# The last tile's products of a conditional-mix and routed low-rank layer, put in another column order

## The chip, the cores and the metric

One core of one Trainium2 chip. The metric is the device time of one execution in microseconds, the median of several. The core's engines run side by side and are tied by semaphores: TensorE (PE) multiplies, VectorE (DVE) and ScalarE (ACT) read its results, GpSimd (POOL) gathers rows, SyncE (SP) issues most transfers.

## The reference

For 64 batches, a matrix `W = weights[condition]` of 32 x 32 mixes the 32 channels of `x` (64, 32, 512). The mixed rows `y` then go through a base layer and a routed low-rank layer, and all of it is added to `x`:

```python
y      = einsum('bct,bcd->bdt', x, weights[condition])       # 64 x 32 x 512
result = einsum('bnd,od->bno', y, W_base) + b_base           # 512 -> 512
logits = einsum('bnd,ed->bne', y, W_gate)                    # 8 experts
route  = top-2 of softmax(logits), renormalised
h      = einsum('bnd,erd->bner', y, A)                       # 8 experts x 16 ranks
delta  = einsum('bner,eor->bno', h * route, B)
out    = x + result + delta
```

## The kernel before

The 2048 rows are cut into 16 tiles of 128 rows (four batches), tile 0 to tile 15 (`LAST`). For a tile, TensorE computes `y` turned, by four products of `x` with a block-diagonal matrix (`mix_tile`, L467, into `y_ps`). ACT copies it into `y_hi` (L271), a type with fewer bits, and DVE takes the rest, `y_lo` (L360). Weights are split in the same way into `w_hi` and `w_lo`. The main products are then three for each of four chunks of 128 features, `y_hi` with `w_hi`, `y_hi` with `w_lo`, and `y_lo` with `w_hi`: 12 steps, all added up in PSUM.

The columns of the weights are laid out as: 256 of the base layer's first half (`BASE`), 64 ranks (`H`), 256 of its second half, 64 ranks, 8 of the gate (`E`), 648 in all (`ALL`). A step takes them in two products, of 320 and of 328 columns (L485), into the two banks of `main_ps[t % 2]`. In this way `main_ps0` belongs to even tiles and `main_ps1` to odd ones, tiles 13 and 15 among these.

DVE routes a tile (`route_tile`: L367 top values, L369 indices, five small steps, L385 the weighted ranks `hw`). TensorE transposes `hw` (`turn`, L495, into `hwT_ps`), ACT copies it into `hwT_hi` (L282), DVE takes the rest into `hwT_lo` (L394), and TensorE adds six low-rank products of 256 columns (`lora`, L505) onto the base columns. DVE adds the bias to `x` beforehand (`add_bias`, L401) and then the sum in `main_ps` to it (`finish`, L407). SP stores the tile (L215).

The order on each engine is written out by hand. On TensorE the work of tile t - 1 stands among the products of tile t: its transposition ahead of step 4, its low-rank products ahead of step 9. The mix products of tile t + 1 stand ahead of the products of tile t. A tile's products wait for `result_ready` of the tile two before, which had the same banks.

The last tile is written apart. Its ranks and gate come first, as 12 side products of 144 columns (L565) into the free `y_ps0`, so that its route can begin early. Then come its base columns, two products of 256 to a step (L571), with the transposition of tile 14 after step 1, the transposition of tile 15 and the low-rank products of tile 14 after step 7, and at the end its own low-rank products, half by half. Two adds (L448) and two stores (L219) of half a tile end the program.

Of the kernel before, what the change touches and what calls it, by code (L numbers as in the profile page):

```python
# [5 lines left out]
def adaln_ffn_kernel(  # L6
# [20 lines left out]
    ALU = mybir.AluOpType  # L27
# [6 lines left out]
    TILES = BATCHES // Q  # L34
    CHUNKS = D // P
    RANKS = b_lora.shape[0]
    E = w_all.shape[1] - D - RANKS
# [6 lines left out]
    BASE, H, G = OUT // 2, RANKS // 2, E // 2  # L44
    HALF = BASE + H
    ALL = 2 * HALF + E
    SIDE = H + E
    LAST = TILES - 1


# [2 lines left out]
    STEPS = len(ORDER)  # L53
    TURN_AT, LORA_AT = 4, 9
    SECOND_MIX_AT = 4
    LAST_TURN_AT = 1, 7
    PICKED = 2


# [7 lines left out]
    with ctx:  # L67
# [108 lines left out]
        result_ready = sem("result_ready")  # L176
        stored = sem("stored")

        def first_halves():

            for h, bank in enumerate((y_ps[0], hwT_ps[0])):
                f = slice(h * D // 2, (h + 1) * D // 2)
                yield bank[:, 0:D // 2], y_hi[0][:, f], y_lo[0][:, f]
# [3 lines left out]
        @block.sync  # L187
        def _(sp):
            def load_x(t):
                sp.dma_start(x_sb[:, t, :], x_tiles[t, :, :]).then_inc(x_landed[t], 16)  # L190

            def load_w(c):
                sp.dma_start(w_raw[:, c, :], w_chunks[c, :, :]).then_inc(w_landed[c], 16)

            sp.dma_start(cond_sb[:, :], cond).then_inc(cond_landed, 16)  # L195
            sp.dma_start(table[:, :, :], cond_w.rearrange("(p k) d -> p k d", k=K)).then_inc(table_landed, 16)
            load_x(0)
            load_w(0)
            load_w(1)
            load_x(1)  # L200
            load_w(2)
            load_w(3)

            sp.wait_ge(mixw_landed[0], 16)
            sp.dma_start(b_raw[:, :], b_lora).then_inc(b_landed, 16)
            load_x(2)
            sp.dma_start(bias_sb[:, :], bias.to_broadcast([P, OUT])).then_inc(bias_landed, 16)
            load_x(3)
            for t in range(LAST):
                if t + 4 < TILES:  # L210

                    sp.wait_ge(y_done, t + 2)
                    load_x(t + 4)
                sp.wait_ge(result_ready, t + 1)
                sp.dma_start(out_tiles[t, :, :], x_sb[:, t, :]).then_inc(stored, 16)  # L215
            for half in range(2):
                n = slice(half * BASE, (half + 1) * BASE)
                sp.wait_ge(result_ready, LAST + half + 1)
                sp.dma_start(out_tiles[LAST, :, n], x_sb[:, LAST, n]).then_inc(stored, 16)  # L219
            sp.wait_ge(stored, 16 * (TILES + 1))  # L220

# [39 lines left out]
        @block.scalar  # L261
        def _(act):
            def split_w(c):
                act.wait_ge(w_landed[c], 16)
                act.activation(w_hi[:, c, :], w_raw[:, c, :], ACT.Copy).then_inc(w_hi_ready, 1)

            def split_y(t):
                act.wait_ge(y_done, t + 1)
                if t >= 2:
                    act.wait_ge(main_done, t - 1)  # L270
                act.activation(y_hi[t % 2][:, :], y_ps[t % 2][:, :], ACT.Copy).then_inc(y_hi_ready, 1)  # L271

            def exp_second(t):
                act.wait_ge(top_ready, t + 1)
                act.activation(second[:, :], top[:, 0:1], ACT.Exp, bias=top[:, 1:2], scale=-1.0)\  # L275
                    .then_inc(second_ready, 1)

            def split_hwT(t):
                act.wait_ge(hwT_done, t + 1)
                if t >= 2:  # L280
                    act.wait_ge(base_done, t - 1)
                act.activation(hwT_hi[t % 2][:, :], hwT_ps[t % 2][:, 0:P], ACT.Copy)\  # L282
                    .then_inc(hwT_hi_ready, 1)

            act.wait_ge(table_landed, 16)
            act.activation(table_split[:, :, 0, :], table[:, :, :], ACT.Copy).then_inc(table_hi_ready, 1)
            split_w(0)
            split_w(1)
            for (y, hi, _), done, ready in zip(first_halves(), (first_y_done, y_done),
                                               (first_y_hi_ready, y_hi_ready)):  # L290
                act.wait_ge(done, 1)
                act.activation(hi, y, ACT.Copy).then_inc(ready, 1)
            split_w(2)
            split_w(3)
            split_y(1)
            act.wait_ge(b_landed, 16)
            act.activation(b_hi[:, :], b_raw[:, :], ACT.Copy).then_inc(b_hi_ready, 1)  # L297

            for t in range(1, TILES):
                exp_second(t - 1)  # L300
                if t == LAST:
                    exp_second(LAST)
                else:
                    split_y(t + 1)
                split_hwT(t - 1)
            split_hwT(LAST)

        @block.vector
        def _(dve):
# [82 lines left out]
            def low_hwT(t):  # L392
                dve.wait_ge(hwT_hi_ready, t + 1)
                dve.tensor_tensor(hwT_lo[t % 2][:, :], hwT_ps[t % 2][:, 0:P], hwT_hi[t % 2][:, :].bitcast(f32),  # L394
                                  ALU.subtract).then_inc(hwT_lo_ready, 1)
# [31 lines left out]
            for t in range(1, TILES):  # L427
                before = main_ps[(t - 1) % 2]
                route_tile(t - 1, before[:, :, BASE:HALF], before[:, 1, HALF:HALF + E])
                if t + 2 < TILES:  # L430
                    select(t + 2)
                if t == LAST:
                    side = y_ps[0][:, 0:2 * SIDE].rearrange("p (h n) -> p h n", h=2)
                    route_tile(LAST, side[:, :, 0:H], side[:, 1, H:SIDE])
                low_hwT(t - 1)
                if t + 1 < TILES:
                    low_y(t + 1)
                add_bias(t - 1)
                if t == LAST:
                    low_hwT(LAST)  # L440
                    add_bias(LAST)
                finish(t - 1)

            dve.wait_ge(xb_ready, TILES)
            for half in range(2):
                n = slice(half * BASE, (half + 1) * BASE)
                dve.wait_ge(base_done, LAST + half + 1)
                dve.tensor_tensor(x_sb[:, LAST, n], main_ps[LAST % 2][:, half, 0:BASE], x_sb[:, LAST, n],  # L448
                                  ALU.add).then_inc(result_ready, 1)

        @block.tensor
        def _(pe):
# [20 lines left out]
                y, w = ((y_hi, w_hi), (y_hi, w_lo), (y_lo, w_hi))[n]  # L473
                return y[t % 2][:, c * P:(c + 1) * P], w[:, c, :]

            def side_columns(w):

                first = w[:, BASE:BASE + SIDE]
                return bass.AP(first.tensor, first.offset, [first.ap[0], [HALF, 2], [1, SIDE]])

            def main_step(t, i, c, n):
                y, w = operands(c, n, t)
                for half in range(2):
# [10 lines left out]
                    pe.wait_ge(hwT_lo_ready, t - 1)  # L494
                pe.transpose(hwT_ps[t % 2][:, 0:P], hw[t % 2][:, :], ident[:, :]).then_inc(hwT_done, 1)  # L495

            def lora(t, by_half=False):
                pe.wait_ge(hwT_lo_ready, t + 1)
                parts = ((hwT_hi, b_hi), (hwT_hi, b_lo), (hwT_lo, b_hi))
                order = [(n, half) for n in range(3) for half in range(2)]  # L500
                if by_half:
                    order.sort(key=lambda x: x[1])
                for n, half in order:
                    h, w = parts[n]
                    last = pe.matmul(main_ps[t % 2][:, half, 0:BASE], h[t % 2][:, :],  # L505
                                     w[:, half * BASE:(half + 1) * BASE],
                                     start=False, stop=n == 2, skip_group_check=True)
                    if (n, half) == order[-1] or by_half and n == 2:
                        last.then_inc(base_done, 1)

            pe.wait_ge(warm_ready, 1)
            warm_up(WARM_BEFORE)
# [45 lines left out]
                    main_step(t, i, c, n)  # L558


            pe.wait_ge(y_lo_ready, TILES)
            side = y_ps[0][:, 0:2 * SIDE].rearrange("p (h n) -> p h n", h=2)
            for i, (c, n) in enumerate(ORDER):
                y, w = operands(c, n, LAST)
                last = pe.matmul(side, y, side_columns(w), start=i == 0, stop=i == STEPS - 1)  # L565
            last.then_inc(main_done, 1)
            pe.wait_ge(result_ready, LAST - 1)
            for i, (c, n) in enumerate(ORDER):
                y, w = operands(c, n, LAST)
                for half in range(2):  # L570
                    pe.matmul(main_ps[LAST % 2][:, half, 0:BASE], y, w[:, half * HALF:half * HALF + BASE],  # L571
                              start=i == 0, stop=i == STEPS - 1)
                if i == LAST_TURN_AT[0]:
                    turn(LAST - 1)
                if i == LAST_TURN_AT[1]:
                    turn(LAST)
                    lora(LAST - 1)
            lora(LAST, by_half=True)


# [33 lines left out]
```

## Time and profile before

| | |
|---|---|
| median of 3 runs | 97.9 us (97.78 to 98.39) |
| the profiled execution | 97.5 us, of which the span of its trace is 95.7 |
| TensorE busy | 90.5 us, 95% of the span |
| DVE busy | 65.6 us, 69% |
| ACT busy | 23.8 us, 25% |
| GpSimd busy | 16.1 us, 17% |
| moved by DMA | 10.65 MB, 111 GB/s over the span |

Busy time of TensorE is counted from modelled ends of its matmuls, which overlap; so its pace is read from the spacing of the matmuls' starts, or from the pieces of the chain of waits. That chain is followed back from the last instruction: at each step to whatever released it, or to the instruction ahead of it on its engine.

### The profile page before, as it was taken

The numbers are of one execution on the slowest core, as the hardware profiler recorded it, in microseconds if no ns is written. First come the engines' busy times: TensorE is split into PE (matmuls) and PEld (weight loads), VectorE is DVE, ScalarE is ACT, GpSimd is POOL, SyncE is SP. The second block draws the span as 40 slices with busy tenths as digits, with TensorE's granted clock in tenths as the row PEclk, the third lists the DMA queues.
The fourth block names the chain that finished last, engine by engine and source line by source line (L and its number), as shares of the span: only waits on it lengthen the run. The fifth ranks groups of instructions, "written<-read, shape, count | busy, mean of one in ns | idle before, by whom it ended". The sixth has DMA issues, their size and how long they took to land.

```text
span 95.7 us, 1847 instructions
## 1 busy us (share of the span) xinstructions
PE 90.5 (95%) x657; PEld 87.6 (92%) x657; DVE 65.6 (69%) x234; ACT 23.8 (25%) x56; POOL 16.1 (17%) x29
## 2 busy tenths in 40 slices
PE   5997998999999999999999999999999999999980
PEld 1387997999999999999999999999999999999970
DVE  3768957767586686767675866867676767668880
ACT  5138433130403131221304031311313040311300
POOL 4384303030303021030303030120300000000000
PEclk9999999999999999999999999999999999999999
DMA  0895483060606233140606051331607020302005
GB/s 13 252 335 218 173 265 124 9 219 9 219 7 147 79 132 101 73 153 0 226 7 219 7 188 38 115 115 52 176 8 219 0 110 0 116 0 110 0 10 209
DMA packets 6361, 10.65 MB, mean 111 GB/s; under 512 B 1009, under 2 KB 1617, under 8 KB 6353
## 3 DMA queue, kind: packets, MB, share of 16 engines
q1 hardware_dynamic: 5904, 10.32, 32.6%
q0 software_dynamic: 448, 0.23, 1.1%
q8 instruction: 5, 0.08, 0.4%
q14 instruction: 4, 0.02, 0.1%
HBM read 6.35 MB, written 4.19 MB: 110 GB/s over the span
## 4 chain that ended last, share of the span: by engine, by line
PE 81%; DMA 10%; DVE 2%; issue 1%; ACT 1%; POOL 0%; SPq 0%; DVEq 0%; POOLq 0%
PE main_ps L485 51%; PE y_ps L467 12%; PE main_ps L505 12%; DMA mixw<-cond_w,row_ids 5%; PE main_ps L571 3%; DMA b_raw<-b_lora 3%; DMA table<-cond_w 2%; PE hwT_ps L495 2%; PE y_ps L565 1%; ACT b_hi L297 1%; POOL table_split L238 0%; DVE x_sb L448 0%; SPq L195 0%; DVE hw L385 0%; DVEq L67 0%
## 5 line engine op out<-in xcount | busy, mean ns | idle before, releaser
L485 PE MATMUL main_ps<-w_lo,y_hi 128*128 128x320 f32 x120 | 28.8, 321 | 0.0
L485 PE MATMUL main_ps<-w_hi,y_hi 128*128 128x320 f32 x120 | 28.8, 320 | 0.0
L485 PE MATMUL main_ps<-w_hi,y_lo 128*128 128x320 f32 x120 | 27.4, 311 | 0.0
L242 POOL DMA_INDIRECT mixw<-cond_w,row_ids x14 | 13.7, 976 | 49.3 <-PE y_ps L467 48.6
L485 PEld LDWEIGHTS main_ps<-w_hi,y_lo 128*128 128x128 f32 x120 | 20.3, 188 | 0.0
L485 PEld LDWEIGHTS main_ps<-w_lo,y_hi 128*128 128x128 f32 x120 | 19.9, 189 | 0.1
L485 PEld LDWEIGHTS main_ps<-w_hi,y_hi 128*128 128x128 f32 x120 | 19.4, 190 | 0.0
L467 PE MATMUL y_ps<-mix,x_sb 128*128 128x128 f32 x124 | 16.6, 276 | 0.6 <-DMA x_sb<-x 0.5
L467 PEld LDWEIGHTS y_ps<-mix,x_sb 128*128 128x128 f32 x124 | 15.6, 191 | 0.8 <-issue 0.7
L275 ACT ACTIVATE second<-top 128x1 f32<-128x1 f32 x16 | 4.7, 296 | 44.3 <-DVE top L367 44.3
L407 DVE TENSOR_TENSOR x_sb<-main_ps,x_sb 128x512 f32<-128x512 f32 x15 | 10.4, 691 | 5.7 <-PE main_ps L505 5.7
L394 DVE TENSOR_TENSOR hwT_lo<-hwT_ps,hwT_hi 128x128 fp32r<-128x128 f32 x16 | 4.7, 292 | 12.8 <-ACT hwT_hi L282 12.8
L401 DVE TENSOR_TENSOR x_sb<-x_sb,bias_sb 128x512 f32<-128x512 f32 x16 | 10.9, 682 | 0.0
L271 ACT ACTIVATE y_hi<-y_ps 128x512 fp32r<-128x512 f32 x15 | 9.0, 598 | 5.5 <-PE y_ps L467 5.5
L360 DVE TENSOR_TENSOR y_lo<-y_ps,y_hi 128x512 fp32r<-128x512 f32 x15 | 10.2, 681 | 0.0
L282 ACT ACTIVATE hwT_hi<-hwT_ps 128x128 fp32r<-128x128 f32 x16 | 4.4, 278 | 10.6 <-PE hwT_ps L495 10.5
L505 PE MATMUL main_ps<-b_hi,hwT_hi 128*128 128x256 f32 x32 | 6.6, 284 | 0.0
L505 PE MATMUL main_ps<-b_hi,hwT_lo 128*128 128x256 f32 x32 | 6.6, 283 | 0.0
L505 PE MATMUL main_ps<-b_lo,hwT_hi 128*128 128x256 f32 x32 | 6.6, 282 | 0.0
L385 DVE SCALAR_TENSOR_TENSOR hw<-main_ps,weight,route 128x128 f32<-128x128 f32 x15 | 5.3, 351 | 0.6
L455 PE MATMUL hwT_ps<-warm 128*128 128x512 bf16 (+1 forms) x12 | 4.3, 484 | 1.2 <-DVE warm L310 1.2
L505 PEld LDWEIGHTS main_ps<-b_hi,hwT_hi 128*128 128x128 f32 x32 | 5.4, 188 | 0.0
(66 smaller groups left out, 77.8 us busy)
## 6 DMA issues: line engine op xcount, KB each, us to landing
x_sb<-x SPq DMA_DIRECT2D x16, 256.0 KB, 2.9
out<-x_sb SPq DMA_DIRECT2D x15, 256.0 KB, 2.0
w_raw<-w_all SPq DMA_DIRECT2D x4, 324.0 KB, 4.6
b_raw<-b_lora SPq DMA_DIRECT2D x1, 256.0 KB, 2.8
bias_sb<-bias SPq DMA_DIRECT2D x1, 256.0 KB, 4.5
out<-x_sb SPq DMA_DIRECT2D x2, 128.0 KB, 1.8
mixw<-cond_w,row_ids POOLq DMA_INDIRECT x14, 2.4
table<-cond_w SPq DMA_DIRECT2D x1, 64.0 KB, 2.0
```

What stands on the lines that cost most here:

```text
L242: pool.indirect_dma_start(mixw[:, t, :], None, cond_w, bass.IndirectOffsetOnAxis(row_ids[:, t:t + 1], 0))\
L271: act.activation(y_hi[t % 2][:, :], y_ps[t % 2][:, :], ACT.Copy).then_inc(y_hi_ready, 1)
L275: act.activation(second[:, :], top[:, 0:1], ACT.Exp, bias=top[:, 1:2], scale=-1.0)\
L282: act.activation(hwT_hi[t % 2][:, :], hwT_ps[t % 2][:, 0:P], ACT.Copy)\
L360: dve.tensor_tensor(y_lo[t % 2][:, :], y_ps[t % 2][:, :], y_hi[t % 2][:, :].bitcast(f32), ALU.subtract).then_inc(y_lo_ready, 1)
L385: dve.scalar_tensor_tensor(out=hw[t % 2][:, :].rearrange("p (h e r) -> p h e r", h=2, e=G), in0=h.rearrange("p h (e r) -> p h e r", e=G), ...
L394: dve.tensor_tensor(hwT_lo[t % 2][:, :], hwT_ps[t % 2][:, 0:P], hwT_hi[t % 2][:, :].bitcast(f32), ALU.subtract).then_inc(hwT_lo_ready, 1)
L401: dve.tensor_tensor(x_sb[:, t, :], x_sb[:, t, :], bias_sb[:, :], ALU.add).then_inc(xb_ready, 1)
L407: dve.tensor_tensor(tile, main_ps[t % 2][:, :, 0:BASE], tile, ALU.add)\
L467: last = pe.matmul(dst, x_sb[:, t, f], mix[t % 2][:, :, :], start=True, stop=True)
L485: last = pe.matmul(main_ps[t % 2][:, half, 0:n_cols], y, w[:, half * HALF:half * HALF + n_cols], start=i == 0, stop=i == STEPS - 1)
L505: last = pe.matmul(main_ps[t % 2][:, half, 0:BASE], h[t % 2][:, :], w[:, half * BASE:(half + 1) * BASE], start=False, stop=n == 2, skip_gr ...
```

## The change

The last tile's 12 steps are done twice, over other columns. In the first pass a step is one product of 392 columns (64 ranks, the second half of the base, 64 ranks, gate) into the second bank of `main_ps1`; in the second pass one of 256 columns (first half of the base) into the first bank. So there are 24 products and not 36, and no column is computed twice. `y_ps0` is no longer used by the last tile. The wait on `result_ready` stands ahead of the first pass. The transposition of tile 14 stands before step 10 of the first pass, the low-rank products of tile 14 before step 5 of the second pass, the transposition of tile 15 before the second pass's last step.

The tile's own low-rank products begin with the second half, and the third of a half alone waits for `hwT_lo`. The last adds and stores take the second half first. On DVE the bias of tile 12 and 13 is added in the turn of tile 13, that of tiles 14 and 15 in the turn of tile 14; the low part of tile 14's `hwT` is taken ahead of the route of tile 15, and the low part of tile 15's behind the sum of tile 14. (DVE's turn t is the pass of its loop that works on tile t - 1's route; "turn of tile 14" is the one that takes `y_lo` of tile 15.)

```diff
@@ sync @@
-            for half in range(2):
+            for i, half in enumerate((1, 0)):
                 n = slice(half * BASE, (half + 1) * BASE)
-                sp.wait_ge(result_ready, LAST + half + 1)
+                sp.wait_ge(result_ready, LAST + i + 1)
                 sp.dma_start(out_tiles[LAST, :, n], x_sb[:, LAST, n]).then_inc(stored, 16)
@@ vector @@
+                low_hwT(t - 1)
                 if t == LAST:
-                    side = y_ps[0][:, 0:2 * SIDE].rearrange("p (h n) -> p h n", h=2)
-                    route_tile(LAST, side[:, :, 0:H], side[:, 1, H:SIDE])
-                low_hwT(t - 1)
+                    route_tile(LAST, last_ranks, last_side[:, SIDE - E:SIDE])
                 if t + 1 < TILES:
                     low_y(t + 1)
-                add_bias(t - 1)
-                if t == LAST:
-                    low_hwT(LAST)
+                if t < LAST - 1:
+                    add_bias(t - 1)
+                if t == LAST - 2:
+                    add_bias(LAST - 2)
+                if t == LAST - 1:
+                    add_bias(LAST - 1)
                     add_bias(LAST)
                 finish(t - 1)
 
+            low_hwT(LAST)
@@ tensor @@
             pe.wait_ge(y_lo_ready, TILES)
-            side = y_ps[0][:, 0:2 * SIDE].rearrange("p (h n) -> p h n", h=2)
-            for i, (c, n) in enumerate(ORDER):
-                y, w = operands(c, n, LAST)
-                last = pe.matmul(side, y, side_columns(w), start=i == 0, stop=i == STEPS - 1)
-            last.then_inc(main_done, 1)
             pe.wait_ge(result_ready, LAST - 1)
             for i, (c, n) in enumerate(ORDER):
                 y, w = operands(c, n, LAST)
-                for half in range(2):
-                    pe.matmul(main_ps[LAST % 2][:, half, 0:BASE], y, w[:, half * HALF:half * HALF + BASE],
-                              start=i == 0, stop=i == STEPS - 1)
-                if i == LAST_TURN_AT[0]:
+                if i == LAST_TURN_AT:
                     turn(LAST - 1)
-                if i == LAST_TURN_AT[1]:
+                last = pe.matmul(last_side, y, w[:, BASE:ALL], start=i == 0, stop=i == STEPS - 1)
+            last.then_inc(main_done, 1)
+            for i, (c, n) in enumerate(ORDER):
+                y, w = operands(c, n, LAST)
+                if i == LAST_LORA_AT:
+                    lora(LAST - 1)
+                if i == OWN_TURN_AT:
                     turn(LAST)
-                    lora(LAST - 1)
-            lora(LAST, by_half=True)
+                pe.matmul(last_base[0], y, w[:, 0:BASE], start=i == 0, stop=i == STEPS - 1)
+            pe.wait_ge(hwT_hi_ready, TILES)
+            for half in (1, 0):
+                n = slice(half * BASE, (half + 1) * BASE)
+                pe.matmul(last_base[half], hwT_hi[LAST % 2][:, :], b_hi[:, n], start=False, stop=False,
+                          skip_group_check=True)
+                pe.matmul(last_base[half], hwT_hi[LAST % 2][:, :], b_lo[:, n], start=False, stop=False,
+                          skip_group_check=True)
+                pe.wait_ge(hwT_lo_ready, TILES)
+                pe.matmul(last_base[half], hwT_lo[LAST % 2][:, :], b_hi[:, n], start=False, stop=True,
+                          skip_group_check=True).then_inc(base_done, 1)
```

On TensorE, at the seam between tile 14 (`y_hi0`, `main_ps0`) and tile 15 (`y_hi1`, `main_ps1`), before:

```order
L485 MATMUL main_ps0<-w_hi,y_lo0 128x328
L565 MATMUL y_ps0<-w_hi,y_hi1 128x144 [waits y_lo_ready]
L565 MATMUL y_ps0<-w_lo,y_hi1 128x144
...
L565 MATMUL y_ps0<-w_hi,y_lo1 128x144
L571 MATMUL main_ps1<-w_hi,y_hi1 128x256 [waits result_ready]
L571 MATMUL main_ps1<-w_hi,y_hi1 128x256
```

And now:

```order
L490 MATMUL main_ps0<-w_hi,y_lo0 128x328
L568 MATMUL main_ps1<-w_hi,y_hi1 128x392 [waits result_ready,y_lo_ready]
L568 MATMUL main_ps1<-w_lo,y_hi1 128x392
...
L568 MATMUL main_ps1<-w_hi,y_hi1 128x392
L500 MATMUL hwT_ps0<-ident,hw0 128x128 [waits hwT_lo_ready,hw_ready]
L568 MATMUL main_ps1<-w_lo,y_hi1 128x392
```

The wait on `result_ready` has moved from behind the twelve side products to the head of the tile.

On TensorE, around tile 15's own transposition (`hw1`), before:

```order
L495 MATMUL hwT_ps1<-ident,hw1 128x128 [waits hwT_lo_ready,hw_ready]
L505 MATMUL main_ps0<-b_hi,hwT_hi0 128x256 [waits hwT_lo_ready]
...
L571 MATMUL main_ps1<-w_hi,y_lo1 128x256 x2
L571 MATMUL main_ps1<-w_hi,y_hi1 128x256 x2
L571 MATMUL main_ps1<-w_lo,y_hi1 128x256 x2
L571 MATMUL main_ps1<-w_hi,y_lo1 128x256 x2
L505 MATMUL main_ps1<-b_hi,hwT_hi1 128x256 [waits hwT_lo_ready]
```

And now:

```order
L576 MATMUL main_ps1<-w_lo,y_hi1 128x256
L500 MATMUL hwT_ps1<-ident,hw1 128x128 [waits hwT_lo_ready,hw_ready]
L576 MATMUL main_ps1<-w_hi,y_lo1 128x256
L580 MATMUL main_ps1<-b_hi,hwT_hi1 128x256 [waits hwT_hi_ready]
L582 MATMUL main_ps1<-b_lo,hwT_hi1 128x256
L585 MATMUL main_ps1<-b_hi,hwT_lo1 128x256 [waits hwT_lo_ready]
```

Between the transposition and the products that need its result fourteen products stood, and one stands now.

On DVE, from `y_lo` of tile 15 (`y_lo1`) on, now:

```order
L402 TENSOR_TENSOR hwT_lo1<-hwT_ps1,hwT_hi1 128x128 [waits hwT_hi_ready]
L368 TENSOR_TENSOR y_lo1<-y_ps1,y_hi1 128x512 [waits y_hi_ready]
L409 TENSOR_TENSOR x_sb<-x_sb,bias_sb 128x512 [waits y_done] x2
L415 TENSOR_TENSOR x_sb<-main_ps1,x_sb 128x512 [waits xb_ready,base_done]
L375 MAX top<-main_ps0 128x8 [waits second_ready,main_done]
```

Before, one bias add (L401) stood where two stand now, ahead of the add that empties tile 13 out of `main_ps1`.

## Rows read from the trace of the kernel before

**Rows 1.** The page: the span, busy time by engine, TensorE's granted clock in 40 slices

```profile
span 95.7 us, 1847 instructions
PE 90.5 (95%) x657; PEld 87.6 (92%) x657; DVE 65.6 (69%) x234; ACT 23.8 (25%) x56; POOL 16.1 (17%) x29
...
PEclk9999999999999999999999999999999999999999
```

**Rows 2.** The chain of waits, 82 us on: start us, us, what

```profile
83.98 1.49 PE main_ps L485 x10
...
87.08 1.30 PE y_ps L565 x12
...
89.01 1.41 PE main_ps L571 x12
...
92.56 0.03 issue
```

**Rows 3.** TensorE's timeline: start us, us, engine line operation out<-in [idle before <-releaser]

```profile
86.92 0.23 PE L565 MATMUL y_ps<-w_hi,y_hi 128*128 128x144 f32 x1
...
90.26 0.27 PE L495 MATMUL hwT_ps<-ident,hw 128*128 128x128 f32 x1
...
92.03 0.28 PE L505 MATMUL main_ps<-b_hi,hwT_hi 128*128 128x256 f32 x1
...
92.62 0.28 PE L505 MATMUL main_ps<-b_hi,hwT_lo 128*128 128x256 f32 x1
```

**Rows 4.** DVE's timeline, 84.5 us on

```profile
84.54 0.68 DVE L360 TENSOR_TENSOR y_lo<-y_ps,y_hi 128x512 fp32r<-128x512 f32 x1
85.14 0.68 DVE L401 TENSOR_TENSOR x_sb<-x_sb,bias_sb 128x512 f32<-128x512 f32 x1
86.23 0.69 DVE L407 TENSOR_TENSOR x_sb<-main_ps,x_sb 128x512 f32<-128x512 f32 x1 [0.41 <-PE main_ps L505]
87.12 0.17 DVE L367 MAX8 top<-main_ps 128x8 f32<-128x8 f32 x1 [0.20 <-PE main_ps L485]
...
88.16 0.35 DVE L385 SCALAR_TENSOR_TENSOR hw<-main_ps,weight,route 128x128 f32<-128x128 f32 x1
...
89.72 0.28 DVE L394 TENSOR_TENSOR hwT_lo<-hwT_ps,hwT_hi 128x128 fp32r<-128x128 f32 x1
89.92 0.68 DVE L401 TENSOR_TENSOR x_sb<-x_sb,bias_sb 128x512 f32<-128x512 f32 x1
90.88 0.29 DVE L394 TENSOR_TENSOR hwT_lo<-hwT_ps,hwT_hi 128x128 fp32r<-128x128 f32 x1 [0.28 <-ACT hwT_hi L282]
...
92.65 0.76 DVE L448 TENSOR_TENSOR x_sb<-main_ps,x_sb 128x256 f32<-128x256 f32 x2 [0.28 <-PE main_ps L505]
```

**Rows 5.** ACT's timeline, tile 15's copy of the transposed ranks

```profile
90.57 0.28 ACT L282 ACTIVATE hwT_hi<-hwT_ps 128x128 fp32r<-128x128 f32 x1 [1.24 <-PE hwT_ps L495]
```

**Rows 6.** Tile 1: timelines of DVE and TensorE around the transposition of tile 0's ranks

```profile
14.52 0.35 DVE L385 SCALAR_TENSOR_TENSOR hw<-main_ps,weight,route 128x128 f32<-128x128 f32 x1
...
14.93 0.33 PE L495 MATMUL hwT_ps<-ident,hw 128*128 128x128 f32 x1 [0.45 <-DVE hw L385]
```

**Rows 7.** SP's timeline: the stores of tiles 13, 14 and of the two halves

```profile
86.95 0.33 SPq L215 DMA_DIRECT2D out<-x_sb  x1
...
92.40 0.33 SPq L215 DMA_DIRECT2D out<-x_sb  x1
...
93.10 0.33 SPq L219 DMA_DIRECT2D out<-x_sb  x1
...
93.48 0.45 SPq L219 DMA_DIRECT2D out<-x_sb  x1
```

**Rows 8.** DMA, GB/s in 40 slices: of 86 to 90 us, of 92.6 to 95.2; landing times

```profile
GB/s 0 0 0 0 0 0 0 0 0 0 0 0 0 0 0 0 0 102 328 369 389 389 410 389 226 21 0 0 0 0 0 0 0 0 0 0 0 0 0 0
...
GB/s 0 0 0 0 0 0 0 0 0 189 221 378 410 410 410 347 378 378 410 284 268 221 378 331 331 347 237 95 142 284 362 362 362 299 190 48 0 0 0 0
...
out<-x_sb SPq DMA_DIRECT2D x2, 128.0 KB, 1.8
```

More of the change, by code:

```diff
@@ L46, in adaln_ffn_kernel @@
     ALL = 2 * HALF + E
-    SIDE = H + E
+    SIDE = H + BASE + H + E
     LAST = TILES - 1
@@ L55, in adaln_ffn_kernel @@
     SECOND_MIX_AT = 4
-    LAST_TURN_AT = 1, 7
+    LAST_TURN_AT, LAST_LORA_AT, OWN_TURN_AT = 10, 5, 11
     PICKED = 2
@@ L177, in adaln_ffn_kernel @@
         stored = sem("stored")
+        last_base = [main_ps[LAST % 2][:, 0, 0:BASE], main_ps[LAST % 2][:, 1, H:H + BASE]]
+        last_side = main_ps[LAST % 2][:, 1, 0:SIDE]
+        first_ranks = last_side[:, 0:H]
+        last_ranks = bass.AP(first_ranks.tensor, first_ranks.offset, [first_ranks.ap[0], [H + BASE, 2], [1, H]])
         def first_halves():
@@ L300, in _ @@
                 exp_second(t - 1)
-                if t == LAST:
-                    exp_second(LAST)
-                else:
+                if t < LAST:
                     split_y(t + 1)
                 split_hwT(t - 1)
+            exp_second(LAST)
             split_hwT(LAST)
@@ L431, in _ @@
                     select(t + 2)
+                low_hwT(t - 1)
                 if t == LAST:
-                    side = y_ps[0][:, 0:2 * SIDE].rearrange("p (h n) -> p h n", h=2)
-                    route_tile(LAST, side[:, :, 0:H], side[:, 1, H:SIDE])
-                low_hwT(t - 1)
+                    route_tile(LAST, last_ranks, last_side[:, SIDE - E:SIDE])
                 if t + 1 < TILES:
                     low_y(t + 1)
-                add_bias(t - 1)
-                if t == LAST:
-                    low_hwT(LAST)
+                if t < LAST - 1:
[4 more added lines that the diff above has]
+                    add_bias(LAST - 1)
                     add_bias(LAST)
                 finish(t - 1)
+            low_hwT(LAST)
             dve.wait_ge(xb_ready, TILES)
-            for half in range(2):
+            for i, half in enumerate((1, 0)):
                 n = slice(half * BASE, (half + 1) * BASE)
-                dve.wait_ge(base_done, LAST + half + 1)
-                dve.tensor_tensor(x_sb[:, LAST, n], main_ps[LAST % 2][:, half, 0:BASE], x_sb[:, LAST, n],
-                                  ALU.add).then_inc(result_ready, 1)
+                dve.wait_ge(base_done, LAST + i + 1)
+                dve.tensor_tensor(x_sb[:, LAST, n], last_base[half], x_sb[:, LAST, n], ALU.add).then_inc(result_ready, 1)
         @block.tensor
@@ L474, in operands @@
                 return y[t % 2][:, c * P:(c + 1) * P], w[:, c, :]
-            def side_columns(w):
-                first = w[:, BASE:BASE + SIDE]
-                return bass.AP(first.tensor, first.offset, [first.ap[0], [HALF, 2], [1, SIDE]])
             def main_step(t, i, c, n):
@@ L495, in turn, with lora @@
                 pe.transpose(hwT_ps[t % 2][:, 0:P], hw[t % 2][:, :], ident[:, :]).then_inc(hwT_done, 1)
-            def lora(t, by_half=False):
+            def lora(t):
                 pe.wait_ge(hwT_lo_ready, t + 1)
[L499 to L509, printed above, removed]
+                for n, (h, w) in enumerate(((hwT_hi, b_hi), (hwT_hi, b_lo), (hwT_lo, b_hi))):
+                    for half in range(2):
+                        last = pe.matmul(main_ps[t % 2][:, half, 0:BASE], h[t % 2][:, :],
+                                         w[:, half * BASE:(half + 1) * BASE],
+                                         start=False, stop=n == 2, skip_group_check=True)
+                last.then_inc(base_done, 1)
             pe.wait_ge(warm_ready, 1)
@@ L569, in _ @@
                 y, w = operands(c, n, LAST)
-                for half in range(2):
-                    pe.matmul(main_ps[LAST % 2][:, half, 0:BASE], y, w[:, half * HALF:half * HALF + BASE],
-                              start=i == 0, stop=i == STEPS - 1)
-                if i == LAST_TURN_AT[0]:
+                if i == LAST_TURN_AT:
                     turn(LAST - 1)
-                if i == LAST_TURN_AT[1]:
-                    turn(LAST)
-                    lora(LAST - 1)
-            lora(LAST, by_half=True)
+                last = pe.matmul(last_side, y, w[:, BASE:ALL], start=i == 0, stop=i == STEPS - 1)
[5 more added lines that the diff above has]
+                if i == OWN_TURN_AT:
+                    turn(LAST)
+                pe.matmul(last_base[0], y, w[:, 0:BASE], start=i == 0, stop=i == STEPS - 1)
[9 more added lines that the diff above has]
+                          skip_group_check=True).then_inc(base_done, 1)
 def kernel(**inputs):
```

## The prediction

> **What bounds the kernel now.** I read the page first: TensorE (PE) is busy 95% of a span of 95.7 us, at a granted clock of full speed, which is the 2.4 GHz level [rows 1]. The chain of waits then says whether that busy time is also the path, and from 82 us on it is: matmuls follow matmuls without a hole until 92.56, and only then come the VectorE (DVE) adds and the stores [rows 2]. So in the stage that the change rewrites, a microsecond off TensorE's queue is a microsecond off the end, and a microsecond that TensorE stands still is one on it. What TensorE waits for, or nearly waits for, is read from the timelines of TensorE, DVE and ScalarE (ACT) in the last 11 us [rows 3, 4, 5].
>
> From the chain I also take the prices. Ten main products of 324 columns on average take 1.49 us, 0.149 each; twelve of 256 columns take 1.41, 0.1175 each; and the twelve side products of 144 columns take 1.30, 0.108 each [rows 2]. The low-rank products have 256 columns too, so six take 0.71. The side products are dear for their width: 144 columns cost nearly what 256 do. Their spacing is that of the weight load, which I therefore price at 0.11 where nothing hides it. A transposition takes 0.11 of the queue in the chain's pieces.
>
> **Sum, part one: the products.** Before, the last tile costs 12 side products (1.30) and 24 of 256 columns (24 x 0.1175 = 2.82, and 0.05 of unevenness), 4.17 in all: from 86.92 to the start of the tile's first low-rank product at 92.03 there are 5.11 us, less two transpositions (0.22) and the six low-rank products of tile 14 (0.71) [rows 2, 3]. After, there are 12 products of 392 columns and 12 of 256. No row has 392 columns. Low bound: no dearer than 324 columns, 0.149. High bound: the slope between 256 and 324 columns, (0.149 - 0.1175) / 68 = 0.00046 a column, carried on for 68 more, 0.181. I take 0.179, since that slope is measured right beside it. That gives 12 x 0.179 + 12 x 0.1175 = 2.15 + 1.41 = 3.56. **Gain 0.61** (low-bound price: 0.97).
>
> The Trainium skill (TensorE: Matmul & The Clock Gate, Back-to-back issue gap) gives N/2.4 + 2.5 ns for an isolated stream, 0.166 for 392 columns and 0.109 for 256. The row for 256 columns shows 0.1175, so this case's trace is dearer than the rule. An estimate by the page alone would make the twelve wide products 0.16 us cheaper than my sum.
>
> **Part two: a wait at the head of the tile.** The side products went to y_ps, which was free, so TensorE went from tile 14 to tile 15 without waiting for anything, and the wait on result_ready stood behind them, long fulfilled. Now the first product writes main_ps1, so it waits for the add that empties tile 13 out of it. Before, that add ran from 86.23 for 0.69, to 86.92 [rows 4]: already just when TensorE wants to start. And it is now later. In tile 14's turn DVE has two bias adds ahead of it in place of one. They are 0.60 apart (84.54, 85.14), so the second starts at 85.74 and the emptying add at 86.34 instead of 86.23; the idle 0.41 before it hides most of the extra add, not all. It ends at 87.03. From DVE's end to TensorE's weight load takes 0.06 (in tile 1 hw ends at 14.87 and TensorE, which stood waiting for it, starts at 14.93 [rows 6]), and the load is exposed, 0.11. First product at 87.20 instead of 86.92: **loss 0.28**. Bounds: 0.11 if the load were hidden and the semaphore free, 0.4 if both are dearer than in tile 1. The same second bias in tile 13's turn costs nothing: between the emptying add and the next tile's max TensorE is what DVE waits for, and TensorE has four mix products (0.9 us) before it needs that result. Queued behind the stalled load are all of the tile's products and both transpositions.
>
> **Part three: DVE's chain, moved.** Tile 14's transposition goes behind ten wide products: 87.20 + 1.79 = 88.99. Its operand hw is ready at 88.51 [rows 4], so no wait. ACT starts 0.31 after a transposition (90.26, 90.57) and DVE's hwT_lo 0.31 after that (90.88) [rows 3, 4, 5]: 89.61. The route of tile 15 now stands behind hwT_lo. It starts 0.20 later, 89.81 (its logits are there at 89.67: last wide product at 89.28, and the 0.39 that lie between a product's start and DVE's at the end, 92.26 to 92.65), and takes 1.39 (87.12 to 88.51), to 91.20; with 0.06, TensorE can load it at 91.26. TensorE meanwhile: the base products start at 88.99 + 0.11 + 2 x 0.179 = 89.46; five of them, six low-rank, six more end at 91.46, and the load for the transposition is wanted one product sooner, 91.34. **No wait, but only 0.08 to spare.** The two bias adds that have left this stretch cost nothing here, before or now; DVE is not the path.
>
> **Part four: the tail.** Before, twelve products stood between tile 15's transposition (90.26) and its own low-rank products (92.03), so ACT and DVE had 1.77 us. Now one product stands there. Transposition 91.46, ACT 91.77 to 92.05, load 92.11, product 92.22; TensorE would be free at 91.69: **loss 0.53**. Then two products, and the third needs hwT_lo: DVE starts at 92.08, 0.29, so 92.37, 0.06, 0.11: 92.54 against 92.46, **loss 0.08**. Bounds for the two together: 0.4 (load hidden) to 0.8. The rest of the order within the tail (b_hi, b_lo, then the low part, half 1 first) costs nothing: the same six products.
>
> **TensorE together**: 0.28 - 0.61 + 0.53 + 0.08 = +0.28; the last product starts at 92.89 instead of 92.62 [rows 3]. What TensorE no longer does, it waits.
>
> **Part five: the stores.** The first half's add starts 0.39 after its last product's start (three products ahead of the one at 92.62, so 92.26, and the add at 92.65), the store goes out 0.45 later, and SP's second store 0.38 behind the first: 93.10 and 93.48 before [rows 3, 4, 7]; now 93.38 and 93.76, **+0.28**. The second add would be ready at 93.68, so SP's pace decides, as before. But the queue is emptier. Before, the store of tile 14 went out at 92.40, and the three streamed in one piece of some 1.7 us, to about 94.9, 1.42 after the last issue [rows 7, 8]. Now tile 14's sum needs the low-rank products that are through at 90.9, and DVE is free at 91.12; its store goes out at 91.8 and is over by 93.5. Alone, a store flows 0.8 after its issue, and 256 KB take 0.8 (87.8 to 88.6 [rows 8]), so 128 KB 0.4 to 0.5: done 1.25 to 1.3 after the issue. **Gain 0.13** (bounds 0 and 0.2). All stores: +0.28 - 0.13 = **+0.15**.
>
> The Trainium skill (DMA: Bandwidth & Descriptors, Anatomy of one DMA — SWDGE (gpsimd) path) puts a constant 2.0 us plus bytes / 436 GB/s on a DMA, mostly the write's receipt, 2.3 for 128 KB. The rows have 1.8 at the median from issue to landing for the halves, behind another store, so that constant is not seen here; an estimate by the rule would leave the gain of 0.13 out, which is the third rival below.
>
> The profiled execution took 97.5 (95.7 of span, 1.8 around it), 0.4 under the median of 97.9. The difference carries over: 97.65 for such an execution, **98.05 for the median, said as 98.0**. About 1% (0.98 us) is what a measurement of this kernel can tell from no change.
>
> **Rivals.** (1) The first wait doesn't bite, because the semaphore comes through before TensorE has drained: 0.28 less, 97.75. Against it: the add ended at 86.92 even without the second bias. Chance 0.10. (2) The tail is hidden too, TensorE never stands: 0.61 less, 97.4. It would need ACT's copy within 0.23 of the transposition; the rows have 0.59. 0.05. (3) The stores get no cheaper: 98.2. For it: the two halves follow each other in the queue as before. 0.14. (4) Slower: DVE's route of tile 15 comes late at its transposition. It decides from 0.08. Route never yet read one bank of main_ps while TensorE wrote the other; if its seven instructions take a third longer, 0.46, then 0.38 pass on, 98.4. Against: the two routes here read different tensors, and the first took 1.39 [rows 4], with TensorE writing another tensor throughout. 0.08. (5) The clock falls to 1.2 GHz in the new gaps: some 10,800 columns of the last tile at 0.42 ns more, +4.5, 102. Against: in tile 1 TensorE stood 0.45 us and the clock stayed at full speed [rows 1, 6]. 0.02. That the change doesn't do what it says is excluded by the order. The forecast holds 0.61.
>
> **Range.** The low prices of the wide products (-0.36) or rival 2 give 97.4 to 97.7; rivals 3 and 4 and the high ends of the waits reach 98.5. 97.4 to 98.5 leaves out about 2 in 10. Faster by over 1% (under 96.9) needs rival 2 and the low price together, 0.03; slower by over 1% (over 98.9) rival 5 or a large rival 4, 0.06; within 1%, 0.91.
>
> **What would show it.** TensorE's timeline: first 392-column product at 87.2, 0.28 behind its predecessor's natural slot, with DVE's emptying add as its releaser; spacing 0.179; an idle stretch of about 0.5 before L580 with ACT's hwT_hi as releaser; last product 92.9. DVE: two bias adds before the emptying add of tile 13; tile 14's sum near 91.1. SP: stores at 91.8, 93.4, 93.8. Wrong it would be if the wide products took 0.15 or less, or if TensorE waited for hw at the last transposition.

## The result, and the profile after

| | before | after |
|---|---|---|
| median of 22 runs each | 97.83 us | 98.28 us |
| span of the profiled execution | 95.7 | 96.2 |
| TensorE busy | 90.5 | 90.6 |
| tile 13's transposition to the start of the last product | 8.91 | 9.23 |
| from there to the end of the span | 3.08 | 3.08 |

The ratio is 1.0049, 95% interval 1.0025 to 1.0072: slower by 0.24 to 0.70 us, within the 1% that was called no change, and inside the range of 97.4 to 98.5. One of the 22 executions after took 115.8 us at a mean granted clock of 0.77; it is left out of the ratio, and the last 9 us, which the change rewrites, are too short to lose 18 us even at half the clock. The forecast difference was +0.15, which lies just below the interval; the part on the prediction says which of its terms did that.

The last two lines of the table are the measures used below. In the first 15 us an execution's length varies for reasons outside the change: over ten profiled executions of ten kernels the first transposition began anywhere from 14.55 to 15.74 us, while from there to tile 13's it always took 68.7 to 68.9. So an effect of 0.1 is read from tile 13's transposition on (83.71 before, 83.89 after), not from the span. Of the span's 0.5 us, 0.18 lie ahead of that point and have nothing to do with the last tile; 0.32 lie behind it. How far such a stretch varies by itself, pairs of kernels with the same order on TensorE show: 8.91 and 8.91 (before and before_bias), 9.23 and 9.23 (after and store_act), 8.30 and 8.30 (late_ranks and late_act), each pair within 0.01.

The page after, its span and busy time by engine:

```profile
span 96.2 us, 1824 instructions
PE 90.6 (94%) x645; PEld 87.2 (91%) x645; DVE 65.4 (68%) x234; ACT 23.8 (25%) x56; POOL 15.9 (17%) x29
```

Twelve products fewer, and TensorE is busy as long as before [rows 1]. The busy time hides the gain because matmuls overlap and their ends are modelled. The chain of waits shows it, piece by piece (start us, us, what):

```profile
86.37 0.90 PE main_ps L490 x6
87.27 0.08 issue
87.34 2.02 PE main_ps L568 x10
89.36 0.11 PE hwT_ps L500
89.47 0.36 PE main_ps L568 x2
...
91.14 0.72 PE main_ps L576 x6
91.86 0.12 PE hwT_ps L500
...
92.00 0.29 ACT hwT_hi L291
...
92.33 0.38 PE main_ps L580
92.72 0.11 PE main_ps L582
92.83 0.23 PE main_ps L585
```

Before, this chain was TensorE without a hole [rows 2]. Now an "issue" stands at 87.27, ACT is on the chain at 92.00, and the piece of ten wide products is 2.02 long though nine spacings of 0.177 and one product are 1.77: the first of them carries a wait. TensorE's timeline at the three places:

```profile
86.81 0.46 PE L490 MATMUL main_ps<-w_hi,y_lo 128*128 128x320 f32 x2
87.34 0.42 PE L568 MATMUL main_ps<-w_hi,y_hi 128*128 128x392 f32 x1
87.60 0.34 PE L568 MATMUL main_ps<-w_lo,y_hi 128*128 128x392 f32 x1
...
91.70 0.27 PE L500 MATMUL hwT_ps<-ident,hw 128*128 128x128 f32 x1
...
92.33 0.38 PE L580 MATMUL main_ps<-b_hi,hwT_hi 128*128 128x256 f32 x1 [0.25 <-ACT hwT_hi L291]
92.55 0.28 PE L582 MATMUL main_ps<-b_lo,hwT_hi 128*128 128x256 f32 x1
92.67 0.38 PE L585 MATMUL main_ps<-b_hi,hwT_lo 128*128 128x256 f32 x1
92.88 0.28 PE L580 MATMUL main_ps<-b_hi,hwT_hi 128*128 128x256 f32 x1
...
93.12 0.28 PE L585 MATMUL main_ps<-b_hi,hwT_lo 128*128 128x256 f32 x1
```

A product that follows a wait is longer in the record (0.42 for 0.34, 0.38 for 0.28), since it is shown from about when its weights start to load; and the idle time in brackets, 0.25, is counted from a modelled end. So the length of a wait is best read forward: the start of the product behind, less one spacing, is where the waiting product really ran. The second wide product starts at 87.60, so the first ran at 87.42; its natural slot was 0.149 behind the last narrow one, 87.10. **Lost 0.32.** In the same way L580 ran at 92.43 and its slot was 91.92: **lost 0.51**. The third low-rank product ran at 92.76 and not at 92.67: **0.09**.

DVE's timeline, to be held against [rows 4] (`hw` of tile 15 is the operand of its transposition):

```profile
85.31 1.28 DVE L409 TENSOR_TENSOR x_sb<-x_sb,bias_sb 128x512 f32<-128x512 f32 x2
86.51 0.69 DVE L415 TENSOR_TENSOR x_sb<-main_ps,x_sb 128x512 f32<-128x512 f32 x1
...
90.02 0.17 DVE L375 MAX8 top<-main_ps 128x8 f32<-128x8 f32 x1
...
91.05 0.35 DVE L393 SCALAR_TENSOR_TENSOR hw<-main_ps,weight,route 128x128 f32<-128x128 f32 x1
...
92.31 0.29 DVE L402 TENSOR_TENSOR hwT_lo<-hwT_ps,hwT_hi 128x128 fp32r<-128x128 f32 x1 [0.32 <-ACT hwT_hi L291]
```

Two bias adds in place of one, no idle time ahead of the emptying add, which ends at 87.20. TensorE's next weight load follows 0.11 later:

```profile
87.31 0.19 PEld L568 LDWEIGHTS main_ps<-w_hi,y_hi 128*128 128x128 f32 x1 [0.32 <-issue]
```

The gain is there as well. From 87.42 to L580's slot at 91.92 are 4.50 us; less two transpositions (0.22) and the low-rank products of tile 14 (0.71) the two passes take 3.57, against the 4.17 of before by the prediction's account: 0.60 saved. 0.32 + 0.51 + 0.09 less 0.60 is the 0.32 of the table.

### The profile page after: what moved, and what is told of

It reads as the page before. It is cut to its first block, busy times and chain, and to the rows that moved or that the text cites. A ratio compares the mean times of both kernels' runs of the same rounds, so it can differ in the third digit from the quotient of the medians.

```text
span 96.2 us, 1824 instructions
## 1 busy us (share of the span) xinstructions
PE 90.6 (94%) x645; PEld 87.2 (91%) x645; DVE 65.4 (68%) x234; ACT 23.8 (25%) x56; POOL 15.9 (17%) x29
## 4 chain that ended last, share of the span: by engine, by line
PE 81%; DMA 10%; DVE 2%; issue 2%; ACT 1%; POOL 0%; SPq 0%; DVEq 0%; POOLq 0%
PE main_ps L490 51%; PE y_ps L477 12%; PE main_ps L506 11%; DMA mixw<-cond_w,row_ids 5%; DMA b_raw<-b_lora 3%; PE main_ps L568 2%; DMA table<-cond_w 2%; PE hwT_ps L500 2%; PE main_ps L576 1%; ACT b_hi L306 1%; POOL table_split L247 0%; DVE x_sb L459 0%; PE main_ps L580 0%; SPq L204 0%; DVE hw L393 0%
## 5 line engine op out<-in xcount | busy, mean ns | idle before, releaser
L506 PE MATMUL main_ps<-b_hi,hwT_lo 128*128 128x256 f32 x30 | 6.0, 283 | 0.0
L506 PE MATMUL main_ps<-b_hi,hwT_hi 128*128 128x256 f32 x30 | 6.0, 282 | 0.0
L506 PE MATMUL main_ps<-b_lo,hwT_hi 128*128 128x256 f32 x30 | 6.0, 282 | 0.0
```

## The experiments

All were timed beside the kernel before on the same chip; the stretches are from one profiled execution each.

| kernel | ratio to before, 95% | tile 13's transposition to last product | from there to the end |
|---|---|---|---|
| before | | 8.91 | 3.08 |
| after | 1.0049 (1.0025 to 1.0072) | 9.23 | 3.08 |
| wait_only | 1.0009 (0.9969 to 1.0049) | 9.14 | 3.08 |
| free_bank | 0.9988 (0.9952 to 1.0024) | 8.90 | 3.07 |
| bias_back | 1.0019 (0.9991 to 1.0047) | 9.19 | 3.08 |
| late_ranks | 0.9952 (0.9923 to 0.9980) | 8.30 | 3.10 |
| turn_10 | 0.9986 (0.9941 to 1.0031) | 9.11 | 3.08 |
| store_act | 0.9984 (0.9939 to 1.0030) | 9.23 | 2.99 |
| before_bias | 1.0000 (0.9956 to 1.0044) | 8.91 | 3.07 |
| late_act | 0.9945 (0.9917 to 0.9974) | 8.30 | 3.05 |

Only the change itself and the two "late" kernels move the time by more than its interval. For the others the stretches decide, and the ratios only say that nothing else of size happened.

**wait_only: the wait alone, in the kernel before**

```diff
             pe.wait_ge(y_lo_ready, TILES)
+            pe.wait_ge(result_ready, LAST - 1)
             side = y_ps[0][:, 0:2 * SIDE].rearrange("p (h n) -> p h n", h=2)
...
             last.then_inc(main_done, 1)
-            pe.wait_ge(result_ready, LAST - 1)
```

> The kernel before with one line moved: the wait on result_ready stands ahead of the twelve side products, which still write y_ps0. Measure: from tile 13's transposition to the start of the last product, 8.91 us before and 9.23 after. Theory (the wait at the head of the tile costs its full length, because TensorE is the path): the emptying add ends as before, 0.1 to 0.12 later the weights load, 0.11 for the load: 0.2 to 0.25 later, so 9.11 to 9.16, and the time 0.2 to 0.25 us longer. Rival (the hole is absorbed by slack behind it): 8.91 and no difference.

9.14. DVE's emptying add and TensorE's weight load for the first side product:

```profile
86.67 0.69 DVE L407 TENSOR_TENSOR x_sb<-main_ps,x_sb 128x512 f32<-128x512 f32 x1 [0.41 <-PE main_ps L505]
...
87.48 0.19 PEld L566 LDWEIGHTS y_ps<-w_hi,y_hi 128*128 128x128 f32 x1 [0.22 <-issue]
```

The add ends at 87.36 and the load begins at 87.48. The 0.23 of this hole stands in full at the last product: nothing behind it absorbs it. The wait at the head of a tile costs even where the add in question isn't late.

**bias_back: one bias add ahead of the emptying add, in the changed kernel**

```diff
+                if t == LAST:
+                    add_bias(LAST - 1)
+                    add_bias(LAST)
                 low_hwT(t - 1)
...
-                if t < LAST - 1:
+                if t < LAST:
                     add_bias(t - 1)
-                if t == LAST - 2:
-                    add_bias(LAST - 2)
-                if t == LAST - 1:
-                    add_bias(LAST - 1)
-                    add_bias(LAST)
```

> The changed kernel with one bias add in tile 14's turn, as before, and those of tiles 14 and 15 in DVE's idle stretch ahead of the low part of tile 14's hwT. Theory: the second bias add is 0.11 of the first wait of 0.32, so 9.12; if the two adds end later than ACT's hwT_hi, up to 0.1 of that comes back at the transposition. Rival (the add's place is of no account, the wait is all the emptying add): 9.23.

9.19, between the 9.12 of the theory and the rival's 9.23, for the reason that the theory had named. From tile 13's transposition to tile 14's it took 5.21 and not 5.31: the second bias add was 0.10 of the first wait. But 0.07 of it came back by tile 15's transposition (7.77 against 7.80). The chain has it in the low-rank products of tile 14, a piece of 0.72 after (at 90.42), and DVE's timeline shows why (the last line is the chain's):

```profile
89.18 1.28 DVE L409 TENSOR_TENSOR x_sb<-x_sb,bias_sb 128x512 f32<-128x512 f32 x2
90.38 0.28 DVE L402 TENSOR_TENSOR hwT_lo<-hwT_ps,hwT_hi 128x128 fp32r<-128x128 f32 x1
...
90.91 0.79 PE main_ps L504 x6
```

The two adds fill what was idle time, and `hwT_lo` starts when they let it, without a wait for ACT; it ends at 90.66, and the first low-rank product of tile 14, which waits for it, has its turn on TensorE at 90.75, less than the 0.16 that a weight load and its wait take. The adds were moved from one place with 0.1 too little room to another.

**free_bank: the wide pass in a bank that nobody has to empty**

```diff
-        last_base = [main_ps[LAST % 2][:, 0, 0:BASE], main_ps[LAST % 2][:, 1, H:H + BASE]]
-        last_side = main_ps[LAST % 2][:, 1, 0:SIDE]
+        last_base = [main_ps[LAST % 2][:, 0, 0:BASE], y_ps[0][:, H:H + BASE]]
+        last_side = y_ps[0][:, 0:SIDE]
...
             pe.wait_ge(y_lo_ready, TILES)
-            pe.wait_ge(result_ready, LAST - 1)
...
             last.then_inc(main_done, 1)
+            pe.wait_ge(result_ready, LAST - 1)
```

> The changed kernel with the 392-column products in y_ps0 instead of main_ps1's second bank, and the wait on result_ready between the two passes. Theory: the first wait (0.32) is gone and everything behind keeps its distances, since only 0.14 of slack lies at tile 15's transposition: 9.23 less 0.32 is 8.91, the time that of the kernel before, ratio 1.000. Rival (DVE's chain sets the time of tile 15's transposition, not TensorE's queue): hw of tile 14 or the order on DVE takes the gain back, 9.1 or more.

8.90, the stretch of the kernel before, and a time that can't be told from it. The chain, from the head of the tile and at the tail:

```profile
87.85 1.77 PE y_ps L567 x10
...
92.27 0.29 ACT hwT_hi L291
...
92.60 0.39 PE y_ps L580
```

Ten wide products now take 1.77 where they took 2.02, and no wait stands ahead of them. The tail is unchanged. So the whole loss against the kernel before is the first wait, and the wait in the tail alone eats what the products save.

**turn_10: tile 15's transposition one product sooner**

```diff
-    LAST_TURN_AT, LAST_LORA_AT, OWN_TURN_AT = 10, 5, 11
+    LAST_TURN_AT, LAST_LORA_AT, OWN_TURN_AT = 10, 5, 10
```

> The changed kernel with tile 15's transposition before step 10 of the second pass in place of step 11. After, its operand was there 0.14 before TensorE loaded it, so one product of 0.12 can change sides. Theory: 9.23 less 0.12 is 9.11, TensorE's wait behind the transposition shorter by 0.12. Rival 4 of the prediction (the operand comes late): TensorE waits ahead of the transposition, 9.23 stays.

9.11, and the chain goes from the base products into the transposition without a wait on DVE:

```profile
91.33 0.60 PE main_ps L576 x5
91.93 0.12 PE hwT_ps L500
...
92.07 0.29 ACT hwT_hi L291
```

The operand was not late. Rival 4 is out, and one product more than the change placed could have stood behind the transposition. Not more: the room ahead of it was 0.14.

**store_act: the last half's store from ACT's queue**

```diff
-            for i, half in enumerate((1, 0)):
-                n = slice(half * BASE, (half + 1) * BASE)
-                sp.wait_ge(result_ready, LAST + i + 1)
-                sp.dma_start(out_tiles[LAST, :, n], x_sb[:, LAST, n]).then_inc(stored, 16)
+            sp.wait_ge(result_ready, LAST + 1)
+            sp.dma_start(out_tiles[LAST, :, BASE:OUT], x_sb[:, LAST, BASE:OUT]).then_inc(stored, 16)
...
             split_hwT(LAST)
+            act.wait_ge(result_ready, LAST + 2)
+            act.dma_start(out_tiles[LAST, :, 0:BASE], x_sb[:, LAST, 0:BASE]).then_inc(stored, 16)
```

> The changed kernel with the last half's store issued from ACT's queue instead of SP's. From the last product's start to the end of the span both kernels take 3.08 us, with 1.84 from the second issue to its landing. Theory (SP's own pace and its longer second issue, 0.44 instead of 0.33, hold the second half back): the flow of the second half begins 0.1 to 0.2 sooner, 2.9 to 3.0. Rival (the write's receipt and the data set the price): 3.03 to 3.08.

2.99 in place of 3.08. SP's store went out at 94.06 and ACT's at 94.40, 0.34 behind it; SP alone needs 0.38:

```profile
94.06 0.33 SPq L226 DMA_DIRECT2D out<-x_sb  x1
...
94.40 0.37 ACTq L314 DMA_DIRECT2D out<-x_sb  x1
```

The theory holds at the weak end of its forecast: 0.04 are the earlier issue and 0.05 a shorter way from the issue to the end. ACT's issue takes 0.37 where SP's second takes 0.44, and by the records of the packets the data then begin 0.52 after the issue's end, as they do from SP. The rest of the last store's price isn't SP's.

**before_bias: the kernel before with the bias adds moved**

```diff
-                add_bias(t - 1)
+                if t < LAST - 1:
+                    add_bias(t - 1)
+                if t == LAST - 2:
+                    add_bias(LAST - 2)
+                if t == LAST - 1:
+                    add_bias(LAST - 1)
+                    add_bias(LAST)
                 if t == LAST:
                     low_hwT(LAST)
-                    add_bias(LAST)
                 finish(t - 1)
```

> The kernel before with the bias adds moved as the change moves them, nothing else. TensorE's order and waits stay, so 8.91. The sum of tile 14 comes 0.33 sooner and its store with it, so that the last three stores no longer flow in one piece. The prediction's view (a freer queue makes the last store 0.1 cheaper): from the last product's start to the end 2.98. The view from the changed kernel's trace (the last store costs 1.84 from issue to landing either way): 3.08.

3.07. The store of tile 14 went out 1.11 ahead of the first half's, at 92.58 (0.70 before [rows 7]), and the flow has a gap (GB/s in 40 slices of 93.2 to 95.8 us; SP's stores):

```profile
GB/s 0 0 0 221 378 347 347 441 378 410 347 410 378 284 95 0 0 0 0 0 126 299 331 410 299 284 174 126 221 331 362 299 410 221 126 16 0 0 0 0
...
92.58 0.33 SPq L215 DMA_DIRECT2D out<-x_sb  x1
93.69 0.81 SPq L219 DMA_DIRECT2D out<-x_sb  x2
```

The queue is free when the halves come, and yet the end comes 0.01 to 0.02 sooner at most. A busy queue was not what made the last store dear. The rate still falls to 126 between the two halves, as it does in the kernels before and after; what the last half waits for there is told in the part on the prediction, under the stores.

**late_ranks: both passes in free banks, and enough work behind the wide pass**

```diff
-    LAST_TURN_AT, LAST_LORA_AT, OWN_TURN_AT = 10, 5, 11
+    LAST_TURN_AT, LAST_LORA_AT, OWN_TURN_AT = 10, 3, 4
...
-        last_base = [main_ps[LAST % 2][:, 0, 0:BASE], main_ps[LAST % 2][:, 1, H:H + BASE]]
-        last_side = main_ps[LAST % 2][:, 1, 0:SIDE]
+        last_base = [y_ps[1][:, 0:BASE], y_ps[0][:, H:H + BASE]]
+        last_side = y_ps[0][:, 0:SIDE]
...
-                finish(t - 1)
+                if t < LAST - 1:
+                    finish(t - 1)
 
+            finish(LAST - 2)
             low_hwT(LAST)
+            finish(LAST - 1)
...
                     if i == LORA_AT:
-                        lora(t - 1)
+                        if t < LAST - 1:
+                            lora(t - 1)
...
-            pe.wait_ge(result_ready, LAST - 1)
...
             last.then_inc(main_done, 1)
+            lora(LAST - 2)
```

> The changed kernel with both passes in free banks (392 columns in y_ps0, 256 in y_ps1), the low-rank products of tile 13 moved from tile 14's step 9 to behind the wide pass, those of tile 14 to the second pass's step 3, tile 15's transposition to step 4, and DVE's sums of tiles 13 and 14 behind the route of tile 15. Theory (all that the change lost again are its waits, and nineteen products behind the wide pass are enough to hide ACT and DVE): no wait on TensorE, 8.91 less 0.47 to 0.61, so 8.3 to 8.45; ratio to the kernel before 0.994 to 0.996. Rival (the wide products themselves cost as much as they save): 8.9, ratio 1.000.

8.30, and a ratio of 0.9952. The chain:

```profile
86.00 1.77 PE y_ps L571 x10
87.77 0.11 PE hwT_ps L503
87.88 0.36 PE y_ps L571 x2
88.24 0.71 PE main_ps L509 x6
...
90.13 0.11 PE hwT_ps L503
90.24 0.96 PE y_ps L580 x8
91.20 0.12 PE y_ps L584
```

No wait, no ACT, no "issue" from the head of tile 15 to its low-rank products. Against the kernel before the stretch is 0.61 shorter, which is the products' saving as the prediction had it, alone and whole. Between tile 15's transposition and the product that needs its result stand eight products, 0.96; one was too few, fourteen (before) more than needed.

**late_act: the same with the last half's store from ACT's queue.** The two edits above together.

> The version with the late low-rank products of tile 13 and free banks, with the last half's store from ACT's queue. Both gains shown so far lie behind each other on the path, so they should add: 8.30 from tile 13's transposition to the last product's start, and 2.99 instead of 3.08 to 3.10 from there to the end; ratio to the kernel before 0.993 to 0.995. If the store of tile 14, which goes out just ahead of the halves here, gets in the way of two queues, the second part stays at 3.1.

8.30 and 3.05, ratio 0.9945. Against late_ranks the end is 0.05 shorter, not the 0.09 to 0.1 that store_act had given. That tile 14's store, which goes out 0.6 ahead of the halves here and 1.6 ahead there, takes the rest is a guess that no run tests; the packets agree as far as they go, for the last three stores flow from 92.90 to 94.50 without the trough that the rate has ahead of the last half wherever SP issues it (shallow in late_ranks, 221 GB/s). The interval overlaps nearly all of that of late_ranks. Both beat the kernel before, and by their ratios to it the changed one too.

## Why the prediction was right, step by step

- **The products** were forecast to save 0.61, with 0.179 for a product of 392 columns. Measured 0.177, and the saving stands alone in late_ranks: 0.61. The slope between two widths in one trace (0.181 if carried on) was good to 0.004 for 68 columns more.
- **The wait at the head**: forecast 0.28, measured 0.32. The emptying add ended where the sum said (87.02 by the clock of before). The 0.04 are the step from its end to the weight load, 0.11 and not the 0.06 of tile 1. wait_only shows 0.12 for it too. In both the product has two waits, and the record of the trace puts the one on `result_ready` on an instruction of its own ahead of the load; the transposition in tile 1 and L580 here, where what is late stands on the load itself, show 0.05 to 0.06. That the order of the two waits would mend it was not tried.
- **The second bias add**: forecast 0.11 of that, measured 0.10 (bias_back).
- **DVE's chain**: no wait at tile 15's transposition, with 0.08 to spare; measured 0.14 to spare, and turn_10 used 0.12 of them without a wait. Rival 4 feared a slower route where DVE reads one bank of `main_ps` while TensorE writes the other: it took 1.38 (90.02 to 91.40), against 1.39 before.
- **The tail**: forecast 0.53 and 0.08, measured 0.51 and 0.09.
- **TensorE together**: forecast +0.28, measured +0.32 (9.23 against 8.91). No large errors cancel in it; the wait at the head is the largest.
- **The stores** is the term that failed. It said that a freer queue makes the last store 0.13 cheaper; measured 0.00 (3.08 and 3.08), which is rival 3. The prediction put 1.25 to 1.3 from the last issue to the end of its data where it had read 1.42 before; by the packets it is 1.47 after and was 1.49 before. The step at fault is the premise that the stores ahead of it held the last half back. They didn't even before: in [rows 8] the rate falls to 95 and 142 from 94.36 to 94.49, so the engines had all but drained when the last half's data began, at 94.45. After, SP's last store and the rate in 40 slices of 93.1 to 95.7 us:

```profile
93.98 0.44 SPq L228 DMA_DIRECT2D out<-x_sb  x1
...
GB/s 410 410 410 315 410 410 221 95 0 0 0 0 0 0 0 0 0 0 0 0 110 205 425 315 315 331 205 111 173 315 362 362 331 284 174 16 0 0 0 0
```

The same trough (111, 173) stands at 94.86 to 94.99. By the traces, what the last half waits for is its own issue. Counted from the end of the issue, the data begin 0.50 to 0.52 later in both halves, before and after: the first half is issued in 0.33 and its data begin 0.84 after the issue's start, the last in 0.45 [rows 7] and 0.44, and its data begin 0.97 and 0.96 after. The data of a half then take 0.52, where the prediction had 0.4 to 0.5. So 0.44 + 0.52 + 0.52 make up the 1.47, and the prediction's 0.8 was that of a store issued in 0.33. before_bias shows the same with TensorE left alone (0.43 + 0.51 + 0.53), and in store_act, with an issue of 0.37, the data of the last half begin 0.52 after its end too, while the first half still flows; that gets 0.05 back. Why SP needs 0.11 more for an issue that follows another by 0.04 stays open.

Without that term the sum is +0.28, 97.8 and 98.2 for the profiled execution and the median, against +0.32 in the trace and 0.24 to 0.70 in the runs. The profiled execution took 98.0 where 97.65 was forecast: 0.18 of that lie ahead of tile 13's transposition, 0.13 in the stores, 0.04 in TensorE's part. The range of 1.1 us would have held any of these; it is the pieces that test the mechanism. Rivals 1 and 2 (a wait that doesn't bite, a hidden tail) are refuted by the two waits in the timeline; rival 4 by the 0.14 to spare; rival 5 by the clock of the profiled execution, which stayed at full speed beside holes of 0.3 and 0.5 us.

## What to carry to other kernels

A rearrangement that saves work on the busiest engine is worth what it saves less the cover that it takes away. Before merging products, count what stands behind each result that another engine must still turn round, and price that way (here 0.31 to ACT, 0.28 for its copy, 0.16 back to the first product) in products; then move work behind it from a neighbour that is in no hurry, as tile 13's low-rank products were. Ask as well which buffer the moved work writes, and who must empty it first: a bank that had been idle since the last mix product was worth 0.32 us. Before a store is called cheaper for an emptier queue, look whether the rate has a trough ahead of its data: if it has, the queue was not what it waited for. Where a kernel's start varies by 1 us, read small effects from a stretch of the trace that begins behind it.

## What the runs showed of the hardware that was not expected

- A store's data begin 0.50 to 0.52 us after the end of its issue, with the transfer engines idle or all but drained. Of two stores of 128 KB issued 0.38 apart by SP, the second's issue takes 0.43 to 0.46 us instead of 0.33, and its data begin later by that much: 0.94 to 0.98 after the issue's start, against 0.83 to 0.85. Issued by ACT, in 0.37, the second costs 0.09 less in all.
- A product whose late semaphore stands on an instruction of its own ahead of the weight load starts to load 0.11 to 0.12 after the releasing engine's end (after, wait_only), against 0.05 to 0.06 where it stands on the load (L580 after, tile 1 before).
- Products of 392 columns follow each other every 0.177 us, of 324 every 0.149, of 256 every 0.1175.
